# Attention and a channel filter on one core: theta and phi's first half ahead of the transposed scores, GpSimd for all of x's low part, g turned in transpose form, ScalarE for theta's second copy

## The reference

```python
theta = einsum('bchw,kc->bkhw', x, theta_w)            # 32 channels
phi   = pool2(einsum('bchw,kc->bkhw', x, phi_w))       # 32 channels, 256 columns after the 2x2 max
g     = pool2(einsum('bchw,kc->bkhw', x, g_w))         # 128 channels, 256 columns
beta  = softmax(theta^T phi, axis=-1)                  # 1024 x 256
o_in  = g beta^T                                       # 128 x 1024
v     = gamma * (o_w o_in) + x
out   = v + toeplitz(filter of 27 taps, circular over the 256 channels) v
```

## Time and profile before

| | before |
|---|---|
| median of 3 runs | 291.29 us (290.26 to 291.39) |
| the profiled execution | 291.25 us |
| its span, first to last instruction | 289.3 us |
| TensorE (PE) busy | 278.7 us, 96% |
| VectorE (DVE) busy | 240.4 us, 83% |
| ScalarE (ACT) busy | 210.5 us, 73% |
| GpSimd (POOL) busy | 145.6 us, 50% |
| granted TensorE clock | 1.0 of full |

### The profile page before, as it was taken

The page is one execution under the profiler, slowest core; times in us unless marked ns, Lnnn a source line. Parts: engine busy times, 40 slices in busy tenths (PEclk is TensorE's granted clock), DMA queues, the critical chain, the costliest instruction groups (busy, mean ns, idle before and its releaser), DMA issues.

```text
span 289.3 us, 4391 instructions
## 1 busy us (share of the span) xinstructions
PE 278.7 (96%) x1246; PEld 218.5 (76%) x1246; DVE 240.4 (83%) x402; ACT 210.5 (73%) x492; POOL 145.6 (50%) x86
## 2 busy tenths in 40 slices
PE   6688999999999999999999999999999999999995
PEld 4365777777877777877778787777777777777873
DVE  6898979798887979888797888879888887988852
ACT  3798676777967687696768769676876967688663
POOL 7056654648364554736456483545648355563200
PEclk9999999999999999999999999999999999999999
DMA  6631847466494636648363674846467484636333
GB/s 206 204 62 28 220 153 205 91 216 138 163 231 152 203 71 228 146 163 229 150 198 66 224 160 162 223 151 199 61 228 165 156 224 146 210 58 189 63 147 145
DMA packets 14057, 46.53 MB, mean 161 GB/s; under 512 B 2513, under 2 KB 3103, under 8 KB 12800
## 3 DMA queue, kind: packets, MB, share of 16 engines
q1 hardware_dynamic: 13692, 46.10, 56.0%
q10 hardware_dynamic: 276, 0.20, 0.2%
q0 software_dynamic: 80, 0.13, 0.1%
HBM read 17.37 MB, written 16.78 MB: 118 GB/s over the span
## 4 chain that ended last, share of the span: by engine, by line
PE 91%; DVE 3%; DMA 2%; ACT 1%; SPq 0%; issue 0%; DVEq 0%
PE psY L831 9%; PE psY L703 6%; PE psV L842 5%; PE psY L842 5%; PE psY L705 5%; PE psY L704 5%; PE psV L728 5%; PE psV L703 5%; PE psV L704 5%; PE psV L705 5%; PE psY L835 5%; PE psY L728 5%; PE psX L768 3%; PE psZ L768 3%; PE psX L782 3%; PE psV L847 3%
## 5 line engine op out<-in xcount | busy, mean ns | idle before, releaser
L358 POOL TENSOR_TENSOR prob_lo<-prob,prob_hi 128x1024 fp32r<-128x1024 f32 x30 | 71.8, 2393 | 93.0 <-ACT prob_hi L433 51.4
L419 ACT ACTIVATE psX<-psX,neg_max 128x256 f32<-128x256 f32 x64 | 28.5, 446 | 39.1 <-DVE neg_max L595 38.7
L345 POOL TENSOR_TENSOR x_lo<-x_raw,x_hi 128x1024 fp32r<-128x1024 f32 x15 | 36.1, 2406 | 10.5 <-DVE theta_aug L546 9.3
L353 POOL CAST x_hi<-x_raw 128x1024 fp32r<-128x1024 f32 x28 | 29.1, 1038 | 17.5 <-DMA x_raw<-x 15.1
L448 ACT COPY y<-psV 128x512 f32<-128x512 f32 x32 | 18.9, 591 | 19.7 <-PE psV L847 19.6
L419 ACT ACTIVATE psZ<-psZ,neg_max 128x256 f32<-128x256 f32 x64 | 29.5, 479 | 0.0
L613 DVE TENSOR_TENSOR theta_aug<-psZ,own_tile 16x512 fp32r<-16x512 f32 x32 | 20.5, 678 | 5.4 <-PE psZ L775 5.4
L831 PE MATMUL psY<-prob_hi,gT_hi 128*128 128x512 f32 x60 | 23.6, 394 | 0.0
L831 PE MATMUL psY<-prob_hi,gT_lo 128*128 128x512 f32 x60 | 23.4, 391 | 0.0
L546 DVE TENSOR_TENSOR theta_aug<-thetaphi,theta_aug 32x512 fp32r<-32x512 f32 x32 | 21.8, 682 | 1.0
L533 DVE TENSOR_REDUCE phi_pool<-thetaphi 32x128 f32<-32x512 f32 x32 | 21.6, 674 | 1.1
(11 more groups left out here) (152 smaller groups left out, 784.9 us busy)
## 6 DMA issues: line engine op xcount, KB each, us to landing
x_raw<-x SPq DMA_DIRECT2D x15, 1024.0 KB, 5.7
out<-y SPq DMA_DIRECT2D x15, 1024.0 KB, 4.0
x_edge<-x_hi SPq DMA_DIRECT2D x64, 104.0 KB
x_edge<-x_lo SPq DMA_DIRECT2D x32, 104.0 KB
theta_aug<-theta_aug SPq DMA_DIRECT2D x30, 64.0 KB, 2.0
x_raw<-x SPq DMA_DIRECT2D x4, 256.0 KB, 4.9
out<-y SPq DMA_DIRECT2D x4, 256.0 KB, 2.1
band_rev<-ring SPq DMA_DIRECT2D x2, 128.0 KB, 4.1
```

Source lines behind the costliest of these rows:

```text
L345: nc.gpsimd.tensor_tensor(x_lo[:, par, :, cols], x_raw[:, par, :, cols], x_hi[:, par, :, cols].bitcast(F32), ALU.subtract).then_inc(x_lo_r ...
L353: nc.gpsimd.tensor_copy(x_hi[:, par, :, cols], x_raw[:, par, :, cols]).then_inc(x_hi_ready[h], 1)
L358: nc.gpsimd.tensor_tensor(prob_lo[:, h], prob[:, h], prob_hi[:, h].bitcast(F32), ALU.subtract).then_inc(prob_lo_ready, 1)
L419: last = nc.scalar.activation(tiles[:, t, :], tiles[:, t, :], ACT.Exp, bias=neg_max[:, col:col + 1], accum_out=exp_sum[:, col:col + 1])
```

## The change

- TensorE: `theta_phi` half 0 of an image moves ahead of both transposed scores: it stood between them at the start of a pass (for n+1) and is now the last item of the pass before. The two transposed scores stand together. `shifts_to_rows` moves from among the attention's last products to behind them, and these products are ordered high parts first.
- g's turning uses `nc.tensor.transpose` in place of a matmul with the identity.
- ScalarE writes theta's second copy in every image; SyncE's DMA copies go, and its load of x follows directly on the store of y. The load is two DMAs, one for each half.
- GpSimd makes `x_lo` of both halves, VectorE none.
- ScalarE takes `take_thetaphi_rest` of half 0 ahead of `probabilities` of half 0. VectorE takes `maxima` of half 0 ahead of `o_in_low` of half 0.
- The two banks of psY are dealt out anew: `tp_o_in_ps` for theta, phi and both attention inputs, `g_out_ps` for g's half 0 and the output's tile 1. `filter_x` (0, 1) waits for g's pooling instead, and `attention_input` half 1 for `o_in_lo_ready[0]`.

```diff
-        shared_ps = psY[:, 1, :]
-        g_o_in_ps = psY[:, 0, :]
+        tp_o_in_ps = psY[:, 1, :]
+        g_out_ps = psY[:, 0, :]
...
         def o_in_bank(i, par, h):
-            if is_last(i, par):
-                return scores_ps[h][:, 0, :]
-            return shared_ps if h == 0 else g_o_in_ps
+            return scores_ps[h][:, 0, :] if is_last(i, par) else tp_o_in_ps
 
         def out_bank(i, par, h, f):
             if f == 0:
                 return turn_ps[par if h == 0 else 1 - par]
-            return g_o_in_ps if h == 1 and is_last(i, par) else shared_ps
+            return tp_o_in_ps if h == 1 and is_last(i, par) else g_out_ps
...
# SyncE
-                sp.dma_start(x_raw[:, par], x_v[2 * i + par]).then_inc(x_loaded[par], 16)
+                for h in range(2):
+                    cols = slice(h * HALF, (h + 1) * HALF)
+                    sp.dma_start(x_raw[:, par, :, cols], x_v[2 * i + par][:, :, cols]).then_inc(x_loaded[h][par], 16)
...
-                if has_next(i, par):
-                    for h in range(2):
-                        copy_theta_high(*following(i, par), h)
...
# GpSimd
-                    x_high(i + 1, par, 0)
-                    x_low_of_half_0(i + 1, par)
-                    x_high(i + 1, par, 1)
+                    for h in range(2):
+                        x_high(i + 1, par, h)
+                        x_low(i + 1, par, h)
...
# ScalarE
                 nc.scalar.copy(theta_aug[0:K, par, cols], thetaphi[0:K, h, :]).then_inc(theta_hi_ready, 1)
-                if is_first(i, par):
-                    nc.scalar.copy(theta_aug[K:2 * K, par, cols], thetaphi[0:K, h, :]).then_inc(first_theta_copy_ready, 1)
+                nc.scalar.copy(theta_aug[K:2 * K, par, cols], thetaphi[0:K, h, :]).then_inc(theta_copied, 1)
...
-                probabilities(i, par, 0)
                 if ahead and not is_first(i, par):
                     take_thetaphi_rest(ni, npar, 0)
+                probabilities(i, par, 0)
                 probabilities_high(i, par, 0)
...
# VectorE
+                maxima(ni, npar, 0)
                 o_in_low(i, par, 0)
-                for h in range(2):
-                    maxima(ni, npar, h)
+                maxima(ni, npar, 1)
...
-                if has_next_but_one(i, par):
-                    x_low_of_half_1(i + 1, par)
...
# TensorE: g_transposed
-                    last = nc.tensor.matmul(gT_bank(i, par)[:, tile], g_pool[:, tile], ident[:], start=True, stop=True)
+                    last = nc.tensor.transpose(gT_bank(i, par)[:, tile], g_pool[:, tile], ident[:])
...
# TensorE: filter_x (0, 1)
-                        pe.wait_ge(o_in_lo_ready[0], upto(1, i, par, 1))
+                        pe.wait_ge(g_pooled, upto(2, *following(i, par), 1))
...
# TensorE: attention_input, half 1
-                    pe.wait_ge(g_pooled, upto(2, *following(i, par), 1))
+                    pe.wait_ge(o_in_lo_ready[0], upto(1, i, par, 1))
...
# TensorE: image
-                scores_transposed(i, par, 0)
-                if not is_first(i, par):
-                    theta_phi(ni, npar, 0)
-                scores_transposed(i, par, 1)
+                for h in range(2):
+                    scores_transposed(i, par, h)
                 theta_phi(ni, npar, 1)
...
-                add_high_attention(i, par, 1, 0)
+                for f in range(CT):
+                    add_high_attention(i, par, 1, f)
+                for f in range(CT):
+                    add_low_attention(i, par, 1, f)
                 shifts_to_rows(ni, npar)
-                add_low_attention(i, par, 1, 0)
-                add_high_attention(i, par, 1, 1)
-                add_low_attention(i, par, 1, 1)
+                if has_next_but_one(i, par):
+                    theta_phi(i + 1, par, 0)
```

More of the change, by code:

```diff
@@ L156, in attention_then_channel_filter @@
         x0_lo_tile_ready = [sem("x0_lo_tile_ready0"), sem("x0_lo_tile_ready1")]
-        x_loaded = [sem("x_loaded0"), sem("x_loaded1")]
+        x_loaded = [[sem(f"x_loaded{h}{par}") for par in range(2)] for h in range(2)]
         x_hi_ready = [sem("x_hi_ready0"), sem("x_hi_ready1")]
@@ L164, in attention_then_channel_filter @@
         theta_hi_ready = sem("theta_hi_ready")
-        first_theta_copy_ready = sem("first_theta_copy_ready")
+        theta_copied = sem("theta_copied")
         x_buffer_free = sem("x_buffer_free")
-        theta_copied = [sem("theta_copied0"), sem("theta_copied1")]
         theta_lo_ready = sem("theta_lo_ready")
@@ L237, in thetaphi_bank @@
         def thetaphi_bank(par, h):
-            return turn_ps[par] if h == 0 else shared_ps
+            return turn_ps[par] if h == 0 else tp_o_in_ps
         def g_bank(par, h):
-            return g_o_in_ps if h == 0 else turn_ps[par]
+            return g_out_ps if h == 0 else turn_ps[par]
         def gT_bank(i, par):
@@ L284, in x_edges @@
                 stack_edges(x_edge[:, par], x_edge_loaded[par], (x_hi[:, par], x_lo[:, par], x_hi[:, par]))
[L286 to L290, removed]
             x_edges(0, 0)
@@ L340, in _, with x_low @@
             pool.dma_start(gamma_sb[:], gamma.partition_broadcast(P)).then_inc(o_loaded, 16)
-            def x_low_of_half_0(i, par):
-                cols = slice(0, HALF)
-                pool.wait_ge(x_hi_ready[0], upto(1, i, par, 1))
+            def x_low(i, par, h):
+                cols = slice(h * HALF, (h + 1) * HALF)
+                pool.wait_ge(x_hi_ready[h], upto(1, i, par, 1))
                 nc.gpsimd.tensor_tensor(x_lo[:, par, :, cols], x_raw[:, par, :, cols],
-                                        x_hi[:, par, :, cols].bitcast(F32), ALU.subtract).then_inc(x_lo_ready[0], 1)
+                                        x_hi[:, par, :, cols].bitcast(F32), ALU.subtract).then_inc(x_lo_ready[h], 1)
             def x_high(i, par, h):
                 cols = slice(h * HALF, (h + 1) * HALF)
-                pool.wait_ge(x_loaded[par], 16 * (i + par))
+                pool.wait_ge(x_loaded[h][par], 16 * (i + par))
                 pool.wait_ge(x_used, upto(2, i, par, h - 3))
@@ L361, in _ @@
             pool.wait_ge(theta_lo_ready, 2)
-            x_low_of_half_0(0, 1)
+            x_low(0, 1, 0)
             pool.wait_ge(band_parts_ready, 1)
             nc.gpsimd.tensor_tensor(band_lo[:], band[:], band_hi[:].bitcast(F32), ALU.subtract).then_inc(band_parts_ready, 1)
-            pool.wait_ge(x_hi_ready[1], 2)
-            nc.gpsimd.tensor_tensor(x_lo[:, 1, :, HALF:HW], x_raw[:, 1, :, HALF:HW], x_hi[:, 1, :, HALF:HW].bitcast(F32),
-                                    ALU.subtract).then_inc(x_lo_ready[1], 1)
+            x_low(0, 1, 1)
             def image(i, par):
@@ L393, in x_high @@
                 cols = slice(h * HALF, (h + 1) * HALF)
-                act.wait_ge(x_loaded[par], 16 * (i + par))
+                act.wait_ge(x_loaded[h][par], 16 * (i + par))
                 nc.scalar.copy(x_hi[:, par, :, cols], x_raw[:, par, :, cols]).then_inc(x_hi_ready[h], 1)
@@ L523, in _ @@
                                     ALU.subtract).then_inc(proj_w_ready, 1)
[L525 to L529, removed]
             def pool2(dst, src):
@@ L718, in theta_phi @@
                 elif h == 1 and not is_first(i, par):
-                    pe.wait_ge(out_evacuated[1][1], upto(1, i, par, -1))
+                    pe.wait_ge(o_in_lo_ready[1], upto(1, i, par, -1))
                 cols = slice(h * HALF, (h + 1) * HALF)
@@ L736, in g_projection @@
                 elif h == 0:
-                    pe.wait_ge(o_in_lo_ready[1], upto(1, i, par, -1))
+                    pe.wait_ge(out_evacuated[1][1], upto(1, i, par, -1))
                 else:
@@ L757, in scores @@
                 pe.wait_ge(theta_lo_ready, upto(2, i, par, h + 1))
[L758 to L761, removed]
+                pe.wait_ge(theta_copied, upto(2, i, par, h + 1))
                 pe.wait_ge(phi_ready, upto(1, i, par, 1))
```

## The result

The changed kernel takes 293.47 us (median of 7 executions, 292.39 to 295.05), the kernel before 291.29 us (290.26 to 292.79 in 7). The ratio is 1.0069, with a 95% interval of 1.0043 to 1.0095: slower by 0.7%, where 0.65% faster (289.4 us) was forecast, and outside the range of 287.8 to 292.4. The profiled execution of the changed kernel took 292.74 us.

A forecast was written before the change was run, and what follows sets the result against it. TensorE was taken as nearly full, with a ScalarE and VectorE chain starting the second scores. From 291.25 us, +0.3 (passes), -0.3 (first pass), +1.0 (last image) and -2.8 (g's turning) gave 289.4 us, range 287.8 to 292.4.

The forecast's parts named there:

- What bounds the kernel: TensorE nearly full, 96% busy; a chain over ScalarE and VectorE sets when the second scores start.
- u: Time in us from the start of the first product of `theta_phi` half 0 in a pass of the changed kernel.
- The bound of TensorE alone: Start of the second scores if only TensorE limited them: 8.65, against 8.91 by the ScalarE and VectorE chain.
- The wait of `filter_x` (0, 1): Product behind the second scores: waiting for g's pooling saves 0.13 + 0.11 us; second half moves `o_in_lo_ready[0]` to `attention_input` half 1.
- The turning: g's turning on TensorE: two transposes for four matmul instructions save 0.18 us an image, 2.8 us in all.
- The last image: Nothing stands between the shifts' matmul and the last image's transposed scores: 1.0 us lost once.
- ScalarE's copies: Two more casts of theta per image, 1.28 us, ahead of `prob` of half 1: no cost, 0.1 us to spare.
- x's low part: Moved from VectorE to GpSimd: ready at about 2.45, wanted by `theta_phi` half 1 at 2.50; no stall, no margin.
- The clock: TensorE's granted clock: no term in the sum, which starts from the earlier kernel's profiled 291.25 us.
- The sum: From 291.25 us: passes +0.3, first pass -0.3, last image +1.0, turning -2.8, giving 289.4 us.
- a late chain ahead of the scores: Rivals: ScalarE's `prob_hi` late, 290.8 to 291.5 us, chance 0.17; GpSimd late with x's low part, about 290.8, chance 0.06.
- slower: Rival: g's transposes drain before the next product, 0.61 in place of 0.37 us, +3.6, 295.8 us; chance 0.08.

The follow-up runs named there:

- e9: e6 with theta's second copy made by SyncE's DMA again in place of ScalarE: 287.01 us, ratio 0.9821 to the kernel before.
- e1: The changed kernel with TensorE adding the high attention parts of both output tiles before the low ones for half 0: 288.92 us, ratio 0.9889.
- e7: The changed kernel with VectorE's old order, the attention input's low part of half 0 ahead of the maxima: 288.73 us, ratio 0.9877.
- e5: e1 with the shifts' matmul back among the attention's products in the pass before the last image alone: 288.04 us, ratio 0.9852.
- e8: e1 with theta's second copy made by SyncE's DMA again in place of ScalarE: 288.89 us, ratio 0.9882.
- e6: e5 with VectorE's pooling of g's half 0 moved behind both low parts of theta: 287.07 us, ratio 0.9816.
- e12: The kernel before with one part of the change alone, ScalarE writing theta's second copy in every image without DMA copies: 297.45 us, ratio 1.0195.
- e11: e1 with the low part of x's half 1 back on VectorE, at the end of its list: 288.93 us, ratio 0.9890.
- e4: The changed kernel with four idle matmuls around the first shifts' matmul: 293.17 us, ratio 1.0033.
- e10: e9 with nine idle matmuls in TensorE's 2.2 us idle stretch ahead of the prologue's first scores: 287.09 us, ratio 0.9838.

## Why the prediction was wrong

- **What bounds the kernel: right.** TensorE, with a chain over ScalarE and VectorE that sets the time of the scores. The rest of half 1 was forecast at u = 3.75, `prob_hi` of half 1 at 7.72, the second scores at 8.91; the trace has 3.76, 7.74 and 8.96. Most of the wait is ahead of the first scores, though, which the prediction didn't look at. The bound of TensorE alone was forecast at 8.65, and e9 has 8.66, but that is luck: 26 products from 2.04 on at 0.23 put the first scores at 8.02 where e9 has them at 8.18, and 0.63 between the scores is the distance of a row that was itself waiting, where e9 has 0.48. The two errors cancel.
- **The step that failed** is the second half of "The wait of `filter_x` (0, 1)". I let `o_in_lo_ready[0]` move to `attention_input` half 1, wanted at u = 11.8, with VectorE there at 10.9. VectorE's time was right (168.01, u = 10.98). The user was not: `add_low_attention` (0, 0) waits for the same semaphore, unchanged by the diff, and stands six products behind the start of `filter_x` (0, 1), at 9.51 + 6 x 0.23 = 10.9. A wait that the change leaves alone became the next to bind when the one ahead of it was taken away. Missed by 0.07 us, it costs 0.24: the product starts 0.13 late and the next one another 0.11. e1 and e7 take it away from either side and show 16.73 us for a pass on the mean. Over 15 passes it is 3.6 us, or 3.8 with the hole's mean of 0.25; the profiled execution missed the forecast by 292.74 - 289.4 = 3.3.
- **The turning: right, and undersized.** 0.37 to 0.14 us, 0.23 saved against 0.18 forecast, so 3.4 against 2.8 us. Two instructions in place of four (TensorE's instructions fall by 32). The Trainium skill ("TensorE: Matmul & The Clock Gate", Terms) has the transpose mode 4 times faster for fp32; the trace agrees in direction only, since a quarter of 0.37 would be 0.09, and 0.14 was measured. The same page's 275 ns for one transpose (Part 4), which it gives for bf16, is no distance between starts here.
- **The last image: right.** 1.0 forecast, 1.00 between the starts in the trace, 0.9 in e5.
- **ScalarE's copies: right for the new order** (e8), with the narrow margin that was given: in e6 VectorE's chain was 0.32 us shorter (theta's low part ends at u = 8.55 in place of 8.87), and only 0.06 of it reached the second scores before `prob_hi` stopped them. For the old order I got it wrong even after the result (e12), by the same kind of oversight: I followed `prob_hi` to the scores, and not the cast that is queued behind it.
- **x's low part: right.** It was ready at 159.43 (u = 2.40) for the third product of `theta_phi` half 1 at 159.61, and e11 shows no cost.
- **The clock: a term that was put at nothing.** The sum starts from an execution of the kernel before at clock 1.0, and the profiled execution of the changed kernel had 0.993. In its trace the first pass takes 17.12 us, 0.12 more than the mean of the others, where in e1, at clock 1.0, it takes 0.05 less: about 0.2 us, an estimate, for the fall at 24 to 27 us.
- **The sum, as it should have been:** 291.25 + 0.3 - 0.3 + 1.0 - 3.4 + 3.6 = 292.4, and 292.6 with the clock; 292.74 was profiled. The rivals had a late chain ahead of the scores, but none behind them, and their "slower" was the transposes. The median lies 0.7 us above the profiled execution. All seven executions were at 0.988 to 0.994, so the clock may have a part in that; no experiment explains it.

## What to carry to other kernels

When a change takes a wait away, list every other instruction that waits for the same semaphore, in program order, and give each its own due time; on a full TensorE an operand that was 0.07 us late cost 0.24 us in each pass. When work is put into an engine's spare time, follow not only its own user but the users of all that is queued behind it. A moved instruction that was covered in a steady loop should be priced once more in the last pass, where its cover is missing, and parts of a change with a certain gain are worth timing alone: one line here gave 1.45% and the whole change took it all back.

## What the runs showed of the hardware that was not expected

Two fp32 transposes of 128 x 128, with the identity, take 0.14 us from their start to the next product's and overlap with the products around them; the same turning as matmuls is four instructions in 0.37 us.

A product whose weight load had to wait is shown 0.50 us long and the next starts 0.34 us after it in place of 0.23, at three different waits (`o_in_lo` at two products, g's pooling at one). The price of a short wait on a full TensorE was thus the delay of the product itself plus 0.11 us.

In 99 of 124 executions of the kernels here, the one before too, the mean granted clock is between 0.987 and 0.994. The traces with such a clock show the lower level for some 3 us (6.7 us in e4, at 0.988), beginning between about 13.8 and 30.0 us; other executions of most of these kernels are at 0.998 to 1.0. Each fall that a trace shows begins near or behind the end of a stretch of idle TensorE; e4 and e10 each fill one of these and don't end the falls. The cause stays open.
